# Order of the score products in the last row of each group of four, in an attention and mixture-of-experts kernel

## The reference, cut to what matters

```python
scores = jnp.einsum('bhid,bhjd->bhij', q, k) / scale
scores = scores + _alibi_bias(N_HEADS, seq_len, M_SLOPE, x.dtype)[None]
attn = jax.nn.softmax(scores, axis=-1)
out = jnp.einsum('bhij,bhjd->bhid', attn, v)
...
x = _layernorm(x + _L0_attn_ref(...), axis=-1)
x = _layernorm(x + _L0_ffn_ref(...), axis=-1)
```

## Time and profile before

| what | value |
|---|---|
| median of 3 runs | 596.89 us (595.86 to 599.13) |
| the profiled execution | 591.68 us, span 589.9 us |
| TensorE busy | 541.4 us (92% of the span) |
| VectorE busy | 405.5 us (69%) |
| ScalarE busy | 341.6 us (58%) |
| GpSimd busy | 220.3 us (37%) |
| mean granted TensorE clock | 0.967 |

### The profile page before, as it was taken

The page is one execution under the profiler, slowest core; times in us unless marked ns, Lnnn a source line. Parts: engine busy times, 40 slices in busy tenths (PEclk is TensorE's granted clock), DMA queues, the critical chain, the costliest instruction groups (busy, mean ns, idle before and its releaser), DMA issues.

```text
span 589.9 us, 12068 instructions
## 1 busy us (share of the span) xinstructions
PE 541.4 (92%) x4594; PEld 309.5 (52%) x4595; DVE 405.5 (69%) x698; ACT 341.6 (58%) x672; POOL 220.3 (37%) x408
## 2 busy tenths in 40 slices
PE   6589999999999999999999999899999459999983
PEld 4334444444445454544445455455666327888873
DVE  2689777787797758789875868988696772222334
ACT  3247676676676867766777766667677112323234
POOL 5736563211225316102550430146012562545560
PEclk9789999999999999999999999999999659999998
DMA  7532342322322433321213333110100103534264
GB/s 165 145 114 88 75 134 66 106 91 76 129 71 71 131 112 134 122 85 48 70 45 79 73 93 102 29 47 26 29 3 20 58 30 76 149 96 136 86 202 143
DMA packets 54793, 52.43 MB, mean 89 GB/s; under 512 B 14116, under 2 KB 43670, under 8 KB 54737
## 3 DMA queue, kind: packets, MB, share of 16 engines
q1 hardware_dynamic: 45824, 34.89, 21.1%
q0 software_dynamic: 6064, 14.83, 8.0%
q10 hardware_dynamic: 2848, 1.97, 1.1%
HBM read 34.10 MB, written 18.16 MB: 89 GB/s over the span
## 4 chain that ended last, share of the span: by engine, by line
PE 74%; DVE 15%; DMA 5%; ACT 2%; issue 2%; POOL 1%; POOLq 0%; ACTq 0%; SPq 0%; DVEq 0%
PE ps L1000 32%; PE ps L1062 17%; DVE row_max L1567 10%; PE ps L1253 6%; PE ps L1267 5%; PE ps L1002 4%; PE ps L1104 1%; DVE heads L1638 1%; DMA max_dram<-max_turned 1%; PE ps L944 1%; PE ps L1209 1%; PE ps L1282 1%; DMA w_nat<-in_qkv_w 1%; PE ps L1122 1%; DMA k_stacks<-k_late 1%
## 5 line engine op out<-in xcount | busy, mean ns | idle before, releaser
L1567 DVE TENSOR_REDUCE row_max<-ps 128x1 f32<-128x1024 f32 x256 | 297.0, 1212 | 87.0 <-PE ps L1000 43.9
L1395 ACT ACTIVATE probs<-ps 128x512 f32<-128x512 f32 x512 | 268.2, 606 | 86.5 <-PE ps L1002 44.5
L1000 PE MATMUL ps<-k_stacks,q_stacks 96*128 96x512 bf16 x448 | 144.8, 388 | 11.8 <-DVE row_max L1567 4.8
L1000 PE MATMUL ps<-q_stacks,k_stacks 99*128 99x512 bf16 (+1 forms) x512 | 140.9, 353 | 0.9 <-ACT probs L1395 0.5
L1062 PE MATMUL ps<-probs,v_unit 128*32 128x256 f32 x2048 | 124.0, 382 | 0.0
L1002 PE MATMUL ps<-distance,slope_eye 128*128 128x128 bf16 x512 | 110.2, 221 | 0.0
L1062 PEld LDWEIGHTS ps<-probs,v_unit 128*32 128x32 f32 x2048 | 60.0, 110 | 51.3 <-issue 9.4
L1000 PEld LDWEIGHTS ps<-k_stacks,q_stacks 96*128 96x128 bf16 x448 | 39.3, 99 | 80.4 <-DVE row_max L1567 29.4
L1000 PEld LDWEIGHTS ps<-q_stacks,k_stacks 99*128 99x128 bf16 x512 | 48.4, 98 | 40.9 <-ACT probs L1395 11.9
L1002 PEld LDWEIGHTS ps<-distance,slope_eye 128*128 128x128 bf16 x512 | 50.2, 98 | 26.0 <-issue 1.9
L705 POOL COPY v_unit<-v_all 128x128 f32<-128x128 f32 (+1 forms) x28 | 8.4, 305 | 120.2 <-PE ps L1062 120.2
(11 more groups left out here) (278 smaller groups left out, 495.5 us busy)
## 6 DMA issues: line engine op xcount, KB each, us to landing
k_stacks<-k_dram SPq DMA_DIRECT2D x46, 144.0 KB
q_stacks<-q_dram SPq DMA_DIRECT2D x46, 72.0 KB
w<-in_w SPq DMA_DIRECT2D x12, 256.0 KB, 2.9
xd<-blank POOLq DMA_DIRECT2D x8, 325.0 KB, 2.7
probs<-xd SPq DMA_DIRECT2D x8, 325.0 KB, 4.0
k_stacks<-in_c_alibi_k SPq DMA_DIRECT2D x24, 96.0 KB
out_dram<-out_t SPq DMA_DIRECT2D x16, 128.0 KB
yt<-zeros POOLq DMA_DIRECT2D x4, 512.0 KB, 3.1
```

What stands on the lines that cost most here:

```text
L1000: mm = pe.matmul(out, lhs, rhs, start=True, stop=at is None)
L1395: act.activation(probs[:, k % KEPT, HALF * e:HALF * (e + 1)], ps[:, ring_of(n), :], ACT.Exp).then_inc(ring_read, 1)
L1567: dve.tensor_reduce(row_max[:, m % 2, i:i + 1], max_pair(k).rearrange("p a n -> p (a n)"), AX.X, ALU.max).then_inc(mx_used, 1)
```

## The change

For row 3 of each group (j = 3 and j = 7 of a unit), E is issued ahead of M; rows 0 to 2 keep M ahead of E. No instruction is added or removed. The last two units (four groups) have no M any more, so 60 of the 64 groups change. VectorE's and ScalarE's programs are the same.

```diff
@@ -1191,11 +1191,15 @@
                             pe.wait_ge(max_loaded[m % SLOTS], 16 * turn_of(m))
                             if m + 2 < UNITS:
                                 pe.wait_ge(loaded[(m + 2) % SLOTS], 16 * loads_by(m + 2))
-                        if m + 2 < UNITS:
+                        last = j % GROUP == GROUP - 1
+                        if m + 2 < UNITS and not last:
                             for h in range(2):
                                 max_half(m + 2, j, h)
                         for e in range(2):
                             exp_half(m, j, e)
+                        if m + 2 < UNITS and last:
+                            for h in range(2):
+                                max_half(m + 2, j, h)
                     for stage, c in hooks(half, (2,)):
                         late(stage, c)
                     if group == 1:
```

## The result

| | before | changed | ratio |
|---|---|---|---|
| median | 596.38 us (595.76 to 599.13, 4 runs) | 616.38 us (612.43 to 619.41, 4 runs) | 1.0329 (95%: 1.0285 to 1.0373) |
| profiled execution, span | 589.9 us | 613.1 us | |

A forecast was written before the change was run, and what follows sets the result against it. TensorE was taken to bound the kernel; a bared wait for a bank adds 28 x 0.24, 32 x 0.30 and 14 x 0.15, together 18.4 us, to the median of 596.89, giving 615.3 us, range 608 to 623.

The forecast's parts named there:

- ordinary groups: Groups without ScalarE's copy of V's result or long late VectorE work: V starts 0.24 or 0.30 us later.
- copying ones: 14 groups where ScalarE also copies out V's result: 0.15 us extra each, 2.1 us together.
- 1 us at most: Some five groups with long late VectorE work pass row 3's reduction delay on: 1 us at most on top.
- What E3b's wait costs a group: TensorE, second half of row 3's E waits for its bank, no longer covered by M: V 0.24 or 0.30 us later.
- Plain: Groups whose exponentials' products have no diagonal products: V starts 0.24 us later, 28 groups, 6.7 us.
- Diagonal: Groups whose exponentials' products have diagonal products: V starts 0.30 us later, 32 groups, 9.6 us.
- The count of the kinds: Changed groups split by what releases V's start: 28 without diagonal products at 0.24 us, 32 others at 0.30 us.
- R3 behind M3 "costs nothing": VectorE's reduction of row 3 follows the later M, costing nothing, with 1.5 us of cover before the next group needs it.
- the clock rival: TensorE's granted clock falls to 0.50 in five long-wait groups, 6 us each, 30 us on top, 645 us; 3%.
- Faster: Rival: row 3's E finds its banks free, 28 groups lose M's 0.20 us wait, 5.6 us gained, 591.3 us; 3%.
- No change: Rival: V's late start is absorbed because something behind it waits anyway, 596.9 us; 4%.

The follow-up runs named there:

- The cut: Changed kernel, two activations of each group, except in the first eight rows, reading 128 of 512 columns: 597.53 us, 1.0015 to the kernel before.
- the half swap: Against the kernel before, only the first half of row 3's E goes ahead of M, the second stays behind it: 597.79 us, 1.0008.
- the first run: Against the kernel before, row 3's E goes ahead of M only in the 30 groups not holding the queries' own key blocks: 604.69 us, 1.0126.
- the old order with the cut: Kernel before, two activations of each group, except in the first eight rows, reading 128 of 512 columns: 594.52 us, 0.9975.
- the row of V as cover: Changed kernel with V's first row (4 of its 16 matmuls) issued between the two halves of row 3's E: 620.18 us, 1.0374 to the kernel before.
- the diagonal groups swapped: Against the kernel before, row 3's E goes ahead of M only in the 30 groups holding the queries' own key blocks: 606.95 us, 1.0172.

## Why the prediction was right, and where it was not

*The sum.* 615.3 us forecast, 616.38 measured; 18.4 us of loss forecast, 20.0 between the medians and 19.7 in the loop. In the loop, 36 ordinary groups lost 9.5 us and the 14 copying ones 6.0, close to their terms. Eight others, late groups for the most part, lost 5.0 us where the terms and the extra "1 us at most" gave about 3, and a wait ahead of one group was 0.8 us shorter. So the mechanism carries the sum, but that it fits this well is in part luck. The profiled spans differ by 23.2 us. The other 3.5 us lie behind the loop; that stretch takes 162.4 to 169.8 us in the twelve profiles, so they say nothing of the change.

*What E3b's wait costs a group.* Right to 0.02 us. Plain: 0.24 expected, 0.22 or 0.23 found in 19 groups (4.3 us). Diagonal: 0.30 expected, 0.30 or 0.31 in 17 groups (5.2 us). The diagonal group at 164.84 us, the counterpart of the earlier trace rows:

```profile
167.91 0.60 ACT L1399 ACTIVATE probs<-ps 128x512 f32<-128x512 f32 x1
...
168.56 0.39 PE L1000 MATMUL ps<-q_stacks,k_stacks 99*128 99x512 bf16 x1
...
168.85 0.60 PE L1000 MATMUL ps<-k_stacks,q_stacks 96*128 96x512 bf16 x2
...
169.43 1.93 PE L1062 MATMUL ps<-probs,v_unit 128*32 128x256 f32 x32
```

The activation ends at 168.51, E3b starts at 168.56. The cut and the half swap show that this wait is the cause, the first by taking the activation's time away, the second by giving the cover back.

*The count of the kinds.* I took the 28 starts of V with an activation as their releaser for the plain groups. They are the first groups of a unit, of both kinds: the one at 67.40 us is among them and is diagonal (4.29 us from M0 to V). There are 30 groups that hold the queries' own blocks and 30 that don't, which changes the sum by 0.1 us only.

*Copying groups.* 0.43 was worked out from a diagonal one and came out at 0.43 in the three such groups without late work near. For plain ones I added the same 0.15 to the ordinary 0.24; the five without late work near lost 0.47 or 0.48, and why it is more was not taken apart. Four late groups of four heads that hold the queries' own blocks lost 0.39 to 0.43, two of them without a copy; I had put those two with the ordinary diagonal ones, though their row 3 has no diagonal product.

*R3 behind M3 "costs nothing".* Right for ordinary groups: after V's start each has the same 1.87 us to the next M0, before and after. R3 started at 163.08, 0.10 us behind V's start (expected 0.1).

*Groups with long late work.* "1 us at most" on top was too little. The five that I had in mind lost 0.39 to 0.61 us, but for one with 1.66; with the ordinary loss taken off that is some 2 us on top. The first group with a V lost 0.48 (the 1.0 us in the expectation of the first run comes out if one counts from M3 of the group ahead, which now stands behind E3). The long one is the clock rival come true in a single place. Windows of the changed kernel around it:

```profile
396.00:399.00 3.00, 2.28 (x22) 1.19 (x14) 2.83 (x8) 1.84 (x4) 1.79 (x4) 1.00 0.16 47
399.00:402.00 3.00, 2.02 (x11) 1.19 (x12) 3.00 (x3) 1.28 (x4) 2.36 (x3) 0.78 0.20 65
402.00:405.00 3.00, 3.00 (x32) 1.37 (x34) 2.09 (x4) 1.01 (x3) 0.56 (x1) 0.65 0.11 26
```

and the same group of the kernel before:

```profile
380.00:383.00 3.00, 1.97 (x15) 1.13 (x14) 2.90 (x6) 2.06 (x4) 1.90 (x4) 1.00 0.23 71
383.00:386.00 3.00, 2.54 (x22) 1.41 (x26) 3.00 (x5) 1.60 (x4) 2.39 (x3) 1.00 0.14 44
```

M2 waits there for a reduction that starts behind a reciprocal of 1.75 us, and R3 of the group ahead, being later, made that idle stretch longer. Timelines of the kernel before, of the changed one and of the old order with the cut, and a window of the last:

```profile
383.44 0.61 PE L1000 MATMUL ps<-k_late,q_stacks 96*128 96x512 bf16 x2 [1.47 <-DVE row_max L1567]
...
399.98 0.60 PE L1000 MATMUL ps<-k_late,q_stacks 96*128 96x512 bf16 x2 [1.71 <-DVE row_max L1571]
...
390.43 0.61 PE L1000 MATMUL ps<-k_late,q_stacks 96*128 96x512 bf16 x2 [1.48 <-DVE row_max L1568]
...
390.00:394.00 4.00, 3.54 (x22) 1.73 (x26) 4.00 (x6) 1.87 (x4) 2.39 (x3) 0.73 0.18 52
```

In the changed kernel the granted clock, at 1.00 until then, was at 0.50 (1.2 GHz) from 401 to 404 us. I had priced a fall at 6 us a group and given it 3%; this one cost about 1.2 us, once: 1.66 less 0.22 for E3b and 0.24 for the longer stretch. That R3's delay is what made the clock fall is not shown. In this group it fell in all five profiles in which the stretch had 1.71 us or more, which speaks for it. But with 1.47 to 1.49 us it stayed at 1.00 in four profiles and fell in a fifth, the old order with the cut, where R3 is not delayed; and in the group at 271.10 us of the kernel before, the clock stayed at 1.00 behind a stretch of 1.92 us with the row of V as cover, and fell behind one of 1.33 with the diagonal groups swapped. So the length of this one stretch does not decide it, and what does stays open. The ordinary groups, with 0.3 us more of waiting each, kept a clock of 1.00. The Trainium skill, "TensorE: Matmul & The Clock Gate", section "A second HAM failure mode: psum-queue depth-cycling", tells of a kernel whose bf16 matmuls of 512 columns go through PSUM banks in turn and whose clock goes up and down with the small idle times between them. In these groups the trace does not agree: between 100 and 200 us the clock is at 1.00, with TensorE busy for 97.77 us.

*An early DMA wait* gave 0.8 us back. In the group at 92.9 us of the kernel before, M0 stands behind the maxima's way through DRAM; the gap was 1.15 us, in the changed kernel 0.34. The write took 6.80 and 6.39 us in these two executions, and the gap is between 0 and 3.5 us in others, so this is chance and no gain of the change. The prediction had no wait here at all: it took the maxima's use to lie a whole unit behind.

*The rivals.* "Faster" asked for banks that come free 0.24 us earlier, and the cut comes near it: plain groups then gain 0.1 us by the new order. "No change" fell with the equal stretches behind V's start. "Clock" came true in one group, at a fifth of its price.

## What to carry to other kernels

An instruction between two users of a small ring is cover, and moving it away bares the ring's wait even if nothing is added: work out, for each product of the new order, when the bank that it needs is released (the reader's start, its duration, and here 0.05 to 0.07 us), not only how busy the reader is. In the half swap, one row's products of other work in the gap covered the wait at no cost that the times show. Before work of another kind is used as cover, measure what the passage to it and back costs.

## What was not expected of the hardware

- Passing from bf16 products to V's f32 ones (32-column stationary operands) takes 0.09 or 0.10 us more than the step, and coming back 0.11 to 0.13 us: 8, 24 and 32 instructions of V took 0.57, 1.43 and 1.87 us to the next product. Whether the type or the width of the stationary operand makes the difference was not tried.
- The write of a unit's maxima to DRAM at about 85 us took 6.80, 6.39, 7.55 and 9.18 us in four profiled executions (before, changed, half swap, old order with the cut). The products behind it came 1.15, 0.34, 2.06 and 3.53 us late; and behind the last two of these waits the granted clock fell to 0.50, which made the next group 1.6 us longer. In the kernel before:

```profile
83.91 6.80 DMA max_dram<-max_turned
90.73 2.13 DMA q_stacks<-max_dram
```

So up to 5 us of the scatter between executions can arise in this place (single times of the kernel before are 595.8 to 599.1 us). The stretch behind the loop scatters too. This is the reason why single groups, not times, settle questions of 2 us here. What made that write slow was not tried.
